# Turning the tiles of x before they are combined, in place of combining them first

## The reference

```python
xn = layernorm(x)                                   # over the 512 features
q = (xn @ wq)    # 32 heads of 128
k, v = ctx @ wk, ctx @ wv                           # 8 key/value heads of 128, each serves 4 query heads
q, k = rope(q), rope(k)
attn = softmax(q k^T / sqrt(128) + mask)            # per sequence, 64 x 64
x = x + tanh(g_xattn) * (attn v reshaped) @ wo
logits = layernorm(x) @ route_w.T                   # 8 experts, the best one is taken, weight = its logit
x = x + tanh(g_ffn) * sum_e weight_e * (layernorm(x) @ A_e.T) @ Bw_e.T
```

## Time and profile before

| | |
|---|---|
| median of three runs | 1137.26 us (1136.19 to 1138.29) |
| the profiled execution's own time | 1136.03 us |
| its span, first to last instruction | 1134.2 us |
| PE, DVE, ACT, POOL busy | 97%, 79%, 55%, 54% of the span |
| granted TensorE clock, mean | 0.995 of full speed |

### The profile page before, as it was taken

The page is one execution under the profiler, slowest core; times in us unless marked ns, Lnnn a source line. Parts: engine busy times, 40 slices in busy tenths (PEclk is TensorE's granted clock), DMA queues, the critical chain, the costliest instruction groups (busy, mean ns, idle before and its releaser), DMA issues.

```text
span 1134.2 us, 17081 instructions
## 1 busy us (share of the span) xinstructions
PE 1101.8 (97%) x5664; PEld 921.2 (81%) x5664; DVE 900.4 (79%) x1413; ACT 626.8 (55%) x1090; POOL 611.1 (54%) x513
## 2 busy tenths in 40 slices
PE   7999999889999999999999999999999999999997
PEld 6788888678888888888888777888888888888775
DVE  7984748877787878877888999787878887877887
ACT  6462446466666666666666545455555555555441
POOL 4751458777777777777754434344434334334320
PEclk9999999989999999999999999999999999999999
DMA  6869945476464646464459745453535353542201
GB/s 226 275 233 359 341 152 210 140 280 233 149 224 150 224 148 216 159 195 181 153 214 375 236 140 163 145 183 117 196 125 191 115 179 104 175 140 75 75 1 75
DMA packets 93510, 206.27 MB, mean 182 GB/s; under 512 B 8816, under 2 KB 41712, under 8 KB 87536
## 3 DMA queue, kind: packets, MB, share of 16 engines
q1 hardware_dynamic: 93424, 205.18, 53.2%
HBM read 122.31 MB, written 82.84 MB: 181 GB/s over the span
## 4 chain that ended last, share of the span: by engine, by line
PE 64%; DVE 12%; POOL 11%; issue 8%; ACT 4%; DMA 0%; DVEq 0%; POOLq 0%; SPq 0%; ACTq 0%
PE attn L873 20%; PE proj L814 17%; PE score L831 7%; PE attn L766 6%; POOL rot L1624 3%; PE score L766 3%; PE turned L766 3%; POOL wq_s L1599 2%; PE turned L842 2%; PE attn L858 2%; PE attn L860 2%; DVE q_r L1102 1%; DVE q_r L1060 1%; DVE row_sum L1131 1%; DVE wo_s L1055 1%
## 5 line engine op out<-in xcount | busy, mean ns | idle before, releaser
L873 PE MATMUL attn<-wo_s,o_s 128*128 128x512 f32 x1536 | 378.5, 395 | 0.8 <-DVE o_s L1151 0.8
L814 PE MATMUL proj<-xB,wq_s 128*128 128x512 f32 x1344 | 337.2, 394 | 4.1 <-ACT copies L1422 2.2
L873 PEld LDWEIGHTS attn<-wo_s,o_s 128*128 128x128 f32 x1536 | 283.7, 188 | 58.4 <-DVE o_s L1151 1.3
L814 PEld LDWEIGHTS proj<-xB,wq_s 128*128 128x128 f32 x1344 | 253.1, 189 | 58.5 <-ACT copies L1422 2.6
L1624 POOL TENSOR_TENSOR rot<-rot,tab 128x512 f32<-128x512 f32 x112 | 169.9, 1517 | 173.3 <-ACT rot L1401 173.0
L831 PEld LDWEIGHTS score<-k_r,q_r 128*128 128x128 f32 x1024 | 123.5, 192 | 14.8 <-DVE q_r L1065 9.2
L1400 ACT ACTIVATE rot<-q_r 64x512 f32<-64x512 f32 x86 | 54.2, 630 | 144.6 <-DVE q_r L1102 139.9
L831 PE MATMUL score<-k_r,q_r 128*128 128x64 f32 x1024 | 122.9, 273 | 4.5 <-DVE q_r L1065 4.5
L1143 DVE TENSOR_TENSOR p_low<-turned,p_high 64x512 fp32r<-64x512 f32 x128 | 88.0, 688 | 42.3 <-ACT p_high L1438 40.3
L1446 ACT ACTIVATE o_s<-attn 128x512 fp32r<-128x512 f32 x128 | 69.8, 595 | 76.2 <-PE attn L860 76.1
L1065 DVE TENSOR_TENSOR q_r<-q_r,rot 128x512 f32<-128x512 f32 x86 | 89.0, 1035 | 17.1 <-POOL rot L1624 11.8
(11 more groups left out here) (195 smaller groups left out, 1680.6 us busy)
## 6 DMA issues: line engine op xcount, KB each, us to landing
wq_kept<-wq_s SPq DMA_DIRECT2D x16, 1792.0 KB, 6.2
wq_s<-wq_kept SPq DMA_DIRECT2D x16, 1792.0 KB, 8.3
v_kept<-vst SPq DMA_DIRECT2D x64, 256.0 KB, 4.6
v_s<-v_kept SPq DMA_DIRECT2D x128, 128.0 KB, 4.9
wo_kept<-wo_s SPq DMA_DIRECT2D x32, 512.0 KB, 3.7
wo_s<-wo_kept SPq DMA_DIRECT2D x32, 512.0 KB, 5.1
k_kept<-kst SPq DMA_DIRECT2D x32, 256.0 KB, 2.0
wq_raw<-in_wq SPq DMA_DIRECT2D x16, 512.0 KB, 5.7
```

Of the source, the lines that this page charges most:

```text
L814: last = e.matmul(dst[:, :], wq_s[:, b % 2, A, s, kt, :], xB[:, B, mv, kt, :], start=(first and kt == 0 and m == 0), stop=(kt == 1 and m = ...
L873: last = e.matmul(attn[bp][:, :], o_s[:, s, bp, h, :], wo_s[n % WO_SLOTS][:, m, :], start=(h == 0 and i == 0), stop=(h == GROUP - 1 and i ...
```

## The change

PE now turns the normalised tiles themselves: four blocks of c0 and four of c1 (8 transposes per pair in place of 14), at the job three after the normalisation. ACT copies the two banks back over the tiles. POOL makes T1 to T4 from the turned tiles one job later, and one job later again (five after the normalisation) ACT and DVE split the seven blocks: now not out of PSUM but out of SBUF (`x_place` and `combined`). The bank `small` is not used for it. What waited for the turns (the next fetch into the place, the first combination of wq, the first fetch of wo, the first use of `x_third` for rotated keys, the first fetch of values) now waits for the low parts. The fetches of the later pairs are written one job later.

```diff
-X_COMBINE, X_TURN, X_PLACES = 1, 4, 3
+X_TURN, X_COMBINE, X_SPLIT, X_PLACES = 3, 4, 5, 3
-X_FETCH = [6, 8, 9] + [n + X_TURN + 1 for n in list(X_BESIDE)[:-X_PLACES]]
+X_FETCH = [6, 8, 9] + [n + X_SPLIT + 1 for n in list(X_BESIDE)[:-X_PLACES]]
@@ x_split: the sources of the split
-            for i, b in enumerate(proj):
-                yield b[:, :].rearrange("p (b k t) -> p b k t", b=2, k=2), [
-                    xB[:, 2 * i:2 * i + 2, part, :, cols] for part in range(2)]
-            yield small[:, 0:2 * P].rearrange("p (b k t) -> p b k t", b=1, k=2), [
-                xB[:, 6:7, part, :, cols] for part in range(2)]
+            c0, c1 = (x_place(w) for w in X_PAIRS[pair])
+            for first, n, src in ((B11, 2, c0[:, :].rearrange("p (b k t) -> p b k t", b=2, k=2)),
+                                  (T1, 2, combined[:, 0:2]), (T3, 2, combined[:, 2:4]),
+                                  (B22, 1, c1[:, 2 * P:].rearrange("p (b k t) -> p b k t", b=1, k=2))):
+                yield src, [xB[:, first:first + n, part, :, cols] for part in range(2)]
@@ SP: fetch_x, and in the same way fetch_raw(0, 1) and fetch_values(0, 1)
-                    e.wait_ge(x_turned, 4 * (no - X_PLACES) + 4)
+                    e.wait_ge(x_low, 4 * (no - X_PLACES) + 4)
@@ PE: turn_x
                 e.wait_ge(ln_done, NORM_NO[X_PAIRS[pair][1]] + 1)
-                for i in range(4):
-                    ...
+                for c, w in enumerate(X_PAIRS[pair]):
                     if X_NO[pair]:
-                        ...
+                        e.wait_ge(x_copied, 2 * X_NO[pair] - 1 + c)
+                    turn(proj[c], 0, x_place(w), cols=KT).then_inc(x_turned, 1)
@@ ACT
+            def x_copies(pair):
+                for c, w in enumerate(X_PAIRS[pair]):
+                    e.wait_ge(x_turned, 2 * X_NO[pair] + c + 1)
+                    e.activation(x_place(w), proj[c][:, :], ACT.Copy).then_inc(x_copied, 1)
             def x_highs(pair):
+                e.wait_ge(x_copied, 2 * X_NO[pair] + 2)
                 for i, (src, (high, low)) in enumerate(x_split(pair)):
-                    e.wait_ge(x_turned, 4 * X_NO[pair] + i + 1)
+                    if i in (1, 2):
+                        e.wait_ge(x_combined, 4 * X_NO[pair] + 2 + i)
@@ POOL: combine_x (which now comes after by_sin of the job), combine_weights(0)
-                e.wait_ge(ln_done, NORM_NO[X_PAIRS[pair][1]] + 1)
+                e.wait_ge(x_copied, 2 * no + 2)
                 if no:
-                    e.wait_ge(x_turned, 4 * no - 1)
+                    e.wait_ge(x_low, 4 * no)
-                        e.wait_ge(x_turned, 4 * len(X_PAIRS))
+                        e.wait_ge(x_low, 4 * len(X_PAIRS))
```

More of the change, by code:

```diff
@@ L386, in build @@
         x1_turned, routed, weighted_turned, mixed = sem("x1_turned"), sem("routed"), sem("weighted_turned"), sem("mixed")
-        gates_ready, x_high, raw_high, wq_high = sem("gates_ready"), sem("x_high"), sem("raw_high"), sem("wq_high")
+        gates_ready, x_copied, x_high = sem("gates_ready"), sem("x_copied"), sem("x_high")
+        raw_high, wq_high = sem("raw_high"), sem("wq_high")
         shifted, exponentials, probs_high, v_high = sem("shifted"), sem("exponentials"), sem("probs_high"), sem("v_high")
@@ L769, in turn_x @@
             def turn_x(pair):
-                c0, c1 = (x_place(w) for w in X_PAIRS[pair])
-                T = combined[:, :, :, :].rearrange("p b k n -> p (b k n)")
                 e.wait_ge(ln_done, NORM_NO[X_PAIRS[pair][1]] + 1)
-                for i in range(4):
-                    b = (proj + [small])[i]
+                for c, w in enumerate(X_PAIRS[pair]):
                     if X_NO[pair]:
[L776 to L784, removed]
+                        e.wait_ge(x_copied, 2 * X_NO[pair] - 1 + c)
+                    turn(proj[c], 0, x_place(w), cols=KT).then_inc(x_turned, 1)
             def product(b, i):
@@ L1233, in _ @@
                     by_cos(ROPE_NO["q", *q], q_tile(*q), q_tile(*q))
-                if n - X_TURN in X_BESIDE:
-                    x_lows(X_BESIDE[n - X_TURN])
+                if n - X_SPLIT in X_BESIDE:
+                    x_lows(X_BESIDE[n - X_SPLIT])
             sum_rows(0)
@@ L1481, in _ @@
                 if n - X_TURN in X_BESIDE:
-                    x_highs(X_BESIDE[n - X_TURN])
+                    x_copies(X_BESIDE[n - X_TURN])
+                if n - X_SPLIT in X_BESIDE:
+                    x_highs(X_BESIDE[n - X_SPLIT])
                 if n == SCORES_AFTER:
@@ L1650, in _ @@
                     raw_low(w)
-                if n - X_COMBINE in X_BESIDE:
-                    combine_x(X_BESIDE[n - X_COMBINE])
                 if n in X_BESIDE:
@@ L1656, in _ @@
                     by_sin(ROPE_NO[JOBS[n]])
+                if n - X_COMBINE in X_BESIDE:
+                    combine_x(X_BESIDE[n - X_COMBINE])
                 if n in ROPE_BESIDE:
```

## The result

The changed kernel takes 1139.08 us (median of 20 runs, 1137.35 to 1140.98); the kernel before took 1136.48 us beside it (20 runs, 1134.70 to 1138.68). The ratio is 1.0024, with a 95% interval of 1.0018 to 1.0031: the change makes the kernel slower by 2.6 us. I had forecast 1133.3 us, with a range that ended at 1137.6. The profiled execution of the changed kernel took 1137.81 us, 1.78 us more than that of before; all that follows explains these 1.8 us instead of the -3.5 that I had summed.

The account below looks back on a forecast made before the run. PE was taken to bound the kernel between about 47 and 188 us. A lead of 0.9 us from the first half plus 2.6 from the second gave 3.5 us, so 1133.3 us, with an 8-in-10 range of 1129.3 to 1137.6.

Parts of the forecast that it names:

- PE's shorter turns: PE between jobs: six fewer transposes save 0.65 us per pair, 2.6 us over the four pairs of the second half.
- The first pair: PE at job 13: the turn falls into the wait for wv, job 13 starts at 45.3 us, 2.9 us gained.
- ACT's copies: ACT, two copies out of PSUM per pair at 0.60 us each: 9.6 us in all on a half idle engine.
- One low part on the lock in this chain: Second k group: one low part meeting POOL moves by_cos of job 22 to 88.0 us, leaving a lead of 0.4.
- the walk: Second k group timed: by_cos of job 22 ends at 86.9 us, leaving 1.5 us of the 4.8 lead.
- The fetch is just no longer hidden, by about 0.5 us: Second k group: the fetch for job 16 goes out at about 55.7 us and lands at 60.3, about 0.5 unhidden.
- The second half: low parts one job later harm nobody: Jobs 32 to 47: DVE at about half load, later low parts delay nothing, four turns give their 2.6 us.
- POOL behind the last pair: POOL's first combination of wq ends at 158.4 us, just before by_sin of job 48: no cost, cover 0.3 us.
- rival 2: Behind job 48: POOL's late combination of wq turns PE's lead into waiting; gain about 0, 1136.8 us; chance 0.18.
- Rival 3: Second k group: six of nine full low parts meet POOL at 1.08 us each, giving 1139.2 us; chance 0.12.

Follow-up runs that it names:

- the second half alone: New way only for the four pairs of jobs 32 to 41, the first four as in the kernel before; 1135.93 us against 1137.88, ratio 0.9984.
- the fourth place: Changed kernel with a place of its own for the fourth pair's x, fetched at job 10 without a wait; 1135.38 us, 0.9991 to the kernel before.
- the first half's new way alone: New way only for the four pairs of jobs 8 to 16, the last four as in the kernel before; 1142.3 us, ratio 1.0044.
- the mixed kernel: New way for the first pair and the last four, old for pairs of jobs 11, 13, 16, second combination tile; 1136.96 us, 0.9998 to the kernel before.
- low parts from PSUM: Changed kernel, low parts of the first four pairs reading zeros from PSUM instead of SBUF; 1135.11 us, 0.9989 to the kernel before.
- small moves of xB: Changed kernel with stores and fetches of xB cut to 64 KB of 1 MB each; 1136.41 us, 0.999 to the kernel before.
- two tiles: Changed kernel with a second tile for the combinations, used in turn for the first four pairs; 1140.49 us, 1.0033 to the kernel before.

## Why the prediction was wrong, point by point

- **PE's shorter turns: right.** Eight transposes take 0.8 us from the first to the next job (49.99 to 50.79), where I had 0.9. With the second half alone, four turns brought 2.65 us; forecast 2.6.
- **The first pair: right.** Job 13 starts at 44.51 without a wait; from job 8 it leads by 2.85 us, forecast 2.9; at job 22 by 4.9, forecast 4.8.
- **ACT's copies: right**, 9.6 us in all, and no wait of PE in the changed kernel is put down to them.
- **"One low part on the lock in this chain": the term that failed in size.** There were four meetings, not one. I took 0.9 us of lead at job 28 on the scale from job 8 and it became -1.6. Taken off the low parts, the lock gives 2.7 us at by_cos of job 22, where I took 1.1 at the lower end. I had even priced one meeting per pair before the walk, but the walk's times have none in them: from by_sin of job 18 to the end of the third pair's low parts they leave just the 2.5 us that these take undisturbed. My reason for "one", that by_sin covers half of the time, left out that POOL's combinations stand there too, released by DVE's own low parts. The norm of the fourth pair meets by_sin as well: 3.07 us for two, 1.89 before.
- **A second wait that the walk did not look at.** I asked only when job 26 gets its bank. Job 23 lost 3.37 us before that at 78 us, and its matmuls ran in 4.33 us. It did not matter in the end, since job 26's wait was the later one and swallowed it.
- **"The fetch is just no longer hidden, by about 0.5 us": a second term too small, about 2.3 us.** The fetch went out at 55.69, as I had worked out (55.7 instead of 49.28), but I set its landing against the 60.02 at which DVE took these statistics before, and DVE, too, had a lead by then: it waited 2.17 us, until 59.03. PE felt that. With the fourth place, where the wait is gone, by_cos of job 22 comes 2.3 us sooner. The lock and the fetch were each taken away alone, never together, so their sum is open.
- **"The second half: low parts one job later harm nobody": the step that failed, 3.4 us.** By its own lines it was right: the kernel with only this part gains its 2.6 us. What failed is that I closed the first half's account at job 28. Of the fetches that now wait for low parts I asked only when their tiles land. I did not ask what stands behind a waiting fetch on SP's queue. I had only the stores of values coming earlier by what PE leads, in a stage with DMA at 0.94. What the runs show in its place: the first half's new way alone takes 3.4 us from this stage, and with less for DMA to move the loss is gone. That the work gets there by the fetches held on the queue, the later ones, fits the queue's lines and the mixed kernel, but no run holds these fetches and changes nothing else.
- **POOL behind the last pair: right, and as thin as said.** POOL's timeline of the changed kernel:

```profile
157.13 0.74 POOL L1588 TENSOR_TENSOR combined<-wq_raw 128x256 f32<-128x256 f32 x1 [4.37 <-DVE xB L1040]
160.24 1.29 POOL L1624 TENSOR_TENSOR rot<-rot,tab 128x512 f32<-128x512 f32 x1 [0.17 <-ACT rot L1399]
```

  The cover that I called 0.3 us was 0.17, and rival 2 did not happen.
- **The sum.** Forecast to measured, job 8 to 28: -0.9 to +1.6 us; job 28 to 48: -2.6 to +0.8. These are 2.5 and 3.4 us of error; job 8's early start by chance took 0.8 back.
- **Rival 3** gave 1139.2 us, and 1139.08 were measured, but not by its mechanism alone: it had job 26 between 2.6 and 5 us late and the second half's gain intact behind it. Job 26 was 0.6 us late (1.4 from job 8), and the rest came through the DMA queue. Its agreement is partly luck. Its price per meeting, 1.08 us, held in this kernel, but price times number did not give the delay: four meetings are 4.4 us of DVE's time and 2.7 us at by_cos of job 22.

What stays open: how much each of the later held fetches costs in the second half. With the low parts from PSUM job 28 to 48 takes 58.8 us, though the first fetch goes out at 56.31, as late as in the changed kernel, and DMA's share is 0.68 from 42 to 62 us. But this is the fourth place's case again: jobs 26 and 27 take 7.2 us, the last of the four held fetches goes out 0.6 us before job 26 as in the changed kernel, and from job 26 to 48 it is 66.0 us, 1.0 less than there and 2.6 more than with the second half alone. Neither run brings the second half back; what they show is that a PE that comes 1.6 us later to job 28 finds most of the wait after job 35 gone.

## What to carry to other kernels

When a step is moved later, ask of every in-order queue that waits for it what stands behind the wait, and follow that into the next stage: here four fetches were held 6 to 12 us longer, 8.8 MB in place of 11.4 were moved by 88 us, and 3.4 us were lost in the stage after it, in which DMA is full. Ask it of each fetch by itself: the first, which leaves the plainest dip, cost that stage nothing where the later ones were early. Before moving operands of DVE from PSUM to SBUF, count every POOL instruction beside it, those too that the move itself releases. Count a stage's time from a start that the runs share: counted from job 28 two runs seemed to have won the second half back, and counted from job 26 they had not. Test a change half by half: the half that pays here (0.16% faster) was hidden by the other.

## What the runs showed of the hardware that I had not expected

- Short waits can cost more than their length. After waits of PE of 3.37 and 2.44 us the next 12 matmuls took 4.33 and 4.36 us (2.88 otherwise), and after waits of 2.17, 2.52 and 2.55 us (low parts from PSUM, small moves of xB, fourth place) the next 24 took 7.3 to 7.4 us (5.60 otherwise), at a granted clock of 0.53 to 0.69 in the mean of 3 to 5 us. But with two tiles the jobs after waits of 2.18 and 2.83 us took 4.54 and 3.01 us, after 3.26 us at 80.50 (small moves of xB) they ran in 3.04 us, after 2.58 at 119.06 in 3.01 at a clock of 1.00, and after 1.23 and 1.07 us as fast. So the length of the one wait does not decide it, and what does these runs leave open. Where the wait behind was covered this cost nothing, elsewhere 1.5 to 1.8 us.
- A meeting of DVE and POOL on two inputs in SBUF cost each of the four low parts of the changed kernel's first half about 1.07 us, whether it is 512 or 256 wide (0.68 to at most 1.78, 0.41 to 1.48). It isn't always this price: in the kernel with two tiles three low parts took 1.21 to 1.23 us, 0.54 more than undisturbed. What sets the two prices these runs don't show.
